# A four-layer graph network with an expert feed-forward part: the table's parts become the stationary operand, and the adjacency streams for four tiles at once

## The chip, the cores and the metric

One core of one Trainium2 chip. The metric is the device time of one execution in microseconds; the kernel before has a median of 3117.78 us over 3 runs (3117.64 to 3121.14). TensorE's matmuls are called PE here, its weight loads PEld, VectorE DVE, ScalarE ACT, GpSimd POOL and SyncE SP.

## The reference

6250 nodes with 256 features, 100000 edges (src, dst). Cut to what matters:

```python
deg = segment_sum(ones, rows) + 1.0;  dinv = rsqrt(deg)[:, None]
h = x @ W_in + b_in
for l in range(4):
    h_scaled = h * dinv
    msg = segment_sum(h_scaled[cols], rows) * dinv
    global_ctx = mean(h, axis=0) @ Wg[l] + bg[l]
    z = relu((h + msg) @ Wl[l] + bl[l] + global_ctx)
    h = (z - mu) * rsqrt(var + EPS) * gamma[l] + beta[l]
```

Behind it stands a feed-forward part: experts are chosen by a softmax of the mean row, two of eight are applied to every row (gelu between two products), then a layernorm. Both parts are added to x.

## The kernel before

**Tiles.** The nodes are T = 49 tiles of P = 128 rows. The gather and sum over edges is done as a product with a dense adjacency A, whose entries are small counts in fp8. A first stage (0 to 510 us) builds A from one-hot matmuls column by column of tiles, stages it in SBUF and writes it to DRAM (`write`, L539), counts degrees (`degrees`, L1491) and computes h = x @ W_in (`product`, L1529). Its last steps on PE are the degrees of column 48, the product and the mean row of tile 48; then DVE reads whether all counts fit (the flag), and the scales of the table follow.

**The table.** `tab` holds h times dinv in two f16 parts per tile, high (256 columns) and low (256 columns), for two layers in turn. ACT writes the high part (L1346 for the first layer, L1337 later), DVE the low part (L896) and raises `tab_ready`.

**The layers.** For each tile n of a layer, `aggregate` (L1628) on PE runs 49 matmuls, with a 128x128 fp8 block of A as the stationary operand (the weights) and 512 columns of `tab` (high and low) as the moving one, into one PSUM bank. The result has nodes on partitions. ACT copies its low half (L1367), DVE adds the halves, scales and adds the own term (h of the node itself) from the table (L982 to L988) into U. PE transposes U (`turn_u`, L1590), ACT and DVE split the transposed U in two f16 parts (L1369, L995), and PE multiplies by the layer's weights in six matmuls of 256 columns (`product_u`, L1598) into bank 4. In time, tile n's transposes stand at step 14 and its product at step 24 of the 49 steps of tile n+1. DVE then computes bias, relu and layernorm (L1004 to L1020), the sum of rows (L901) and the new table's low part (L896). In the last layer DVE writes h + x instead (L1029) and takes moments and a normalised row sum of the tile before (`moments`, `normal`, L948 and L958).

```python
for m in range(T):
    ...
    ins = mm(acc[a][:, :], A_s[:, a, m, :], tab[:, here + m, :], start=m == 0, stop=m == T - 1)
```

**What sets the order.** The order on each engine is written out by hand, with semaphores between engines. The first tile of a layer waits for the table; before its last step stands `mean` (L1608, four f32 matmuls), behind it `context` (L1620); in the first layer `mean` also waits for the bound of the layer weights (`wmax_set`). SP's queue first loads the layer weights (L551 to L554), then A's tiles, 784 KB each, into a ring of three buffers and one for the first tile (L563). Its requests are served in their order. Before the first product PE waits for `wx_ready`, which DVE raises when the layer weights are split in two f16 parts (L936 to L939). The routing behind the layers begins on PE at L1692 and L1695; L1695 waits for the last row sum of DVE.

Of the kernel before, what the change touches and what calls it, by code (L numbers as in the profile page):

```python
# [20 lines left out]
F16 = mybir.dt.float16  # L21
BF16 = mybir.dt.bfloat16
# [25 lines left out]
PK = 5  # L48
# [14 lines left out]
SEVEN = 7  # L63
assert T % SEVEN == 0
# [15 lines left out]
BEFORE_T, BEFORE_MM = 14, 24  # L80
# [28 lines left out]
def build(nc, x, src, dst, W_in, b_in, Wl, bl, Wg, bg, gamma, beta, Wr, br, W1, b1, W2, b2, fgamma, fbeta, out):  # L109
# [4 lines left out]
    AG = nc.dram_tensor("adjacency_general", [FIELDS * PK, PLANES, P, T, P], BF16).ap()  # L114
    ctx = ExitStack()
    with ctx:
# [53 lines left out]
        src_col = sb("src_col", [P, COLS])  # L170
        src_w = sb("src_w", [P, COLS])
# [5 lines left out]
        RW = 11136  # L177
# [32 lines left out]
        Abuf = work((RING + 1) * T * P // 4)  # L210
        A_s = Abuf.bitcast(F8).rearrange("p (a m s) -> p a m s", m=T, s=P)
        A32_s = Abuf.bitcast(I32).rearrange("p (a w) -> p a w", a=RING + 1)
        AG_s = Abuf.bitcast(BF16).rearrange("p (a m s) -> p a m s", m=T, s=P)
        U = work(RING * D).rearrange("p (a f) -> p a f", f=D)
        uT = work(D).bitcast(F16).rearrange("p (a k n) -> p a k n", k=KC, n=P)
        at[0] += (RING + 1) * D

        Wl_s = region[:, at[0]:at[0] + LAYERS * KC * D].rearrange("p (l k f) -> p l k f", l=LAYERS, k=KC)
        at[0] -= (RING + 1) * D
        gT = region[:, at[0]:at[0] + RING * SUPW].rearrange("p (b n) -> p b n", n=SUPW)  # L220
        gx = Abuf[:, 0:2 * TOP * FC * SUPW].bitcast(F16).rearrange("p (b a f n) -> p b a f n", b=2, a=2, n=SUPW)
        assert RING * SUPW <= (RING + 4) * D
        lo_f = work((RING + 1) * D).rearrange("p (a f) -> p a f", f=D)
        acc_s, hs, Q, Z, Zn, Zg, hf = (work(D) for _ in range(7))
        mean_s = work(D).rearrange("p (k n) -> p k n", k=KC)
        xb = work(RING * D).rearrange("p (a f) -> p a f", f=D)
        bg_s = region[:, (RING + 1) * T * P // 4:(RING + 1) * T * P // 4 + LAYERS * D].rearrange("p (l f) -> p l f", f=D)
        assert at[0] <= RW and LAYERS * D == (RING + 1) * D
        Wsq = U[:, 0:KC, :]

        xnb = sb("xnb", [P, D])
# [46 lines left out]
        c_read = sb("c_read", [P, T])  # L278
        c_own = sb("c_own", [P, T])
        c_back = sb("c_back", [P, LAYERS * T])  # L280
        node = sb("node", [P, T])
# [167 lines left out]
        block = ctx.enter_context(nc.Block())  # L449

        CX = 2
        CT = 9
        CE = 4
        CF = 8
        OUT_PER = [16 * (LOOP + 1), 16 * LOOP, 16 * LOOP]
# [1332 lines left out]
```

## Time and profile before

| | us |
|---|---|
| median of the runs | 3117.78 |
| the profiled execution, its own time | 3118.73 |
| its span, first to last instruction | 3117.1 |
| PE busy | 2988.8 |
| DVE busy | 1943.9 |
| ACT busy | 949.2 |
| mean granted clock of TensorE | 0.976 of full speed |

A PE matmul's duration (380 ns for 512 columns) is its latency; matmuls overlap, and the distance between starts is what a stream costs. A timeline row merges several instructions of a kind: its first number is the start, the second the length, xN the number of them, and in brackets stands the idle time before it with what ended it.

### The profile page before, as it was taken

How to read it: one execution, taken by the hardware profiler on the slowest of the kernel's cores; microseconds unless marked ns; L12 is line 12 of the kernel's file. 1: busy time of each engine (PE TensorE's matmuls, PEld its weight loads, DVE VectorE, ACT ScalarE, POOL GpSimd, SP SyncE). 2: the span in 40 equal slices, each digit the busy share in tenths (PEclk: the TensorE clock that was granted, in tenths of full speed). 3: DMA queues.
4: the chain of work that ended last, by engine and by line, in shares of the span. 5: the costliest groups of instructions: out<-in, count | busy, mean ns of one | idle time of the engine just before them, and what ended most of it. 6: DMA issues, size and time to landing. Idle time of an engine off the chain costs nothing.

```text
span 3117.1 us, 55195 instructions
## 1 busy us (share of the span) xinstructions
PE 2988.8 (96%) x18038; PEld 1702.5 (55%) x18038; DVE 1943.9 (62%) x5237; ACT 949.2 (30%) x2112; POOL 81.6 (3%) x169
## 2 busy tenths in 40 slices
PE   6999996999999999999999999999999999997998
PEld 5777774444444444444444444444444444445887
DVE  8999997555555555555554555545566666666776
ACT  5888897111111111111111111111111111116775
POOL 0000000000000000000000000000000000000111
PEclk9999997999999999999999999999999999998999
DMA  4333334222222221222212221222122222211000
GB/s 132 87 88 88 85 89 137 78 86 86 85 82 86 86 77 65 72 72 72 71 63 72 72 69 65 72 72 72 64 82 84 84 84 75 81 50 40 27 25 26
DMA packets 138138, 233.87 MB, mean 75 GB/s; under 512 B 13718, under 2 KB 105989, under 8 KB 138019
## 3 DMA queue, kind: packets, MB, share of 16 engines
q1 hardware_dynamic: 131058, 217.55, 21.5%
q10 hardware_dynamic: 4608, 8.39, 0.9%
q0 software_dynamic: 2352, 6.40, 0.7%
q8 instruction: 68, 1.11, 0.1%
q14 instruction: 52, 0.42, 0.0%
HBM read 186.58 MB, written 45.74 MB: 75 GB/s over the span
## 4 chain that ended last, share of the span: by engine, by line
PE 83%; ACT 10%; DVE 4%; issue 3%; DVEq 0%; ACTq 0%; DMA 0%; SPq 0%; POOL 0%; POOLq 0%
PE bank L1647 66%; ACT tab L1270 8%; PE bank L1605 4%; PE bank L1749 4%; PE bank L1732 4%; PE bank L1595 1%; PE bank L1495 1%; DVE later L812 1%; DVE region L779 1%; PE bank L1515 1%; PE bank L1541 1%; ACT later L1294 0%; ACT xnb L1288 0%; PE bank L1709 0%; PE bank L1526 0%
## 5 line engine op out<-in xcount | busy, mean ns | idle before, releaser
L1647 PE MATMUL bank<-tab,region 128*128 128x512 f16 x9604 | 2142.3, 380 | 15.8 <-DMA region<-adjacency 15.8
L1647 PEld LDWEIGHTS bank<-tab,region 128*128 128x128 fp8e4 x9604 | 940.6, 98 | 1066.2 <-DVE tab L896 18.0
L1270 ACT ACTIVATE tab<-later 128x539 fp8e4<-128x539 uint8 x588 | 336.2, 674 | 1.9 <-DVE later L812 1.9
L779 DVE TENSOR_SCALAR region<-iota_w,src_col,src_w 128x540 bf16<-128x540 int16 x858 | 310.5, 413 | 0.4 <-issue 0.2
L1373 ACT ACTIVATE sd<-mv,eps_c 128x1 f32<-128x1 f32 x196 | 57.7, 295 | 811.3 <-DVE mv L1011 811.3
L1004 DVE SCALAR_TENSOR_TENSOR region<-bank,c_back,later 128x256 f32<-128x256 f32 x196 | 94.8, 484 | 331.5 <-PE bank L1605 331.5
L995 DVE TENSOR_TENSOR region<-bank,region 128x256 f16<-128x256 f32 x196 | 83.2, 425 | 287.8 <-ACT region L1369 287.8
L1369 ACT ACTIVATE region<-bank 128x256 f16<-128x256 f32 x196 | 75.3, 384 | 568.1 <-PE bank L1595 568.1
L1367 ACT ACTIVATE region<-bank 128x256 f32<-128x256 f32 x196 | 75.3, 384 | 305.1 <-PE bank L1647 305.1
L1605 PE MATMUL bank<-later,region 128*128 128x256 f16 x1176 | 160.4, 273 | 0.9 <-DVE region L995 0.9
L1337 ACT ACTIVATE tab<-region,c_write 128x256 f32 (+1 forms) x147 | 74.6, 508 | 268.7 <-DVE region L1020 268.7
L1732 PE MATMUL bank<-tab 128*128 128x384 f16 (+1 forms) x816 | 139.0, 325 | 7.0 <-DVE tab L1126 4.6
L1605 PEld LDWEIGHTS bank<-later,region 128*128 128x128 f16 x1176 | 115.0, 98 | 56.0 <-DVE region L995 1.2
L1749 PE MATMUL bank<-tab,region 128*128 128x256 f16 (+1 forms) x1176 | 140.5, 277 | 0.0
L984 DVE TENSOR_TENSOR region<-bank,region 128x256 f32<-128x256 f32 x196 | 83.2, 425 | 86.9 <-ACT region L1367 86.9
L1515 PE MATMUL bank<-region 128*128 128x270 bf16 x900 | 132.8, 303 | 1.3 <-DVE region L763 0.8
L1515 PE MATMUL bank<-region,later 128*128 x864 | 125.8, 303 | 1.1 <-DVE region L779 1.1
L1749 PEld LDWEIGHTS bank<-tab,region 128*128 128x128 f16 (+1 forms) x1176 | 118.1, 101 | 15.1
L1515 PEld LDWEIGHTS bank<-region 128*128 128x128 f16 x900 | 109.9, 146 | 20.3 <-DVE region L779 1.6
L1515 PEld LDWEIGHTS bank<-region,later 128*128 128x128 f16 x864 | 111.4, 144 | 12.7 <-issue 1.6
L1137 DVE SCALAR_TENSOR_TENSOR region<-region,g_scale 128x384 f16<-128x384 f32 (+1 forms) x136 | 80.5, 594 | 54.4 <-ACT region L1440 54.2
L1732 PEld LDWEIGHTS bank<-tab 128*128 128x128 f16 x816 | 90.0, 114 | 43.8 <-issue 8.1
(235 smaller groups left out, 2425.1 us busy)
## 6 DMA issues: line engine op xcount, KB each, us to landing
region<-adjacency SPq DMA_DIRECT2D x196, 784.0 KB, 4.3
adjacency<-tab SPq DMA_DIRECT2D x12, 3136.0 KB, 13.7
region<-in_x POOLq DMA_DIRECT2D x48, 128.0 KB, 2.3
out<-region SPq DMA_DIRECT2D x48, 128.0 KB, 1.7
tab<-in_x SPq DMA_DIRECT2D x5, 1024.0 KB, 11.9
dstf<-in_L_ffn_W ACTq DMA_DIRECT2D x16, 256.0 KB, 2.6
srcf<-in_L_ffn_W ACTq DMA_DIRECT2D x16, 256.0 KB, 2.9
tab<-in_L_ffn_W SPq DMA_DIRECT2D x4, 512.0 KB, 4.8
```

Of the source, the lines that this page charges most:

```text
L779: v.tensor_scalar(hot_s[:, j, :], iota_w[:, 0:WP], src_col[:, ds(first_block[0] + j, 1)], src_w[:, ds(first_block[0] + j, 1)], ALU.is_equa ...
L984: tile_own.done(v.tensor_tensor(acc_s, acc[a][:, 0:D], lo_f[:, a, :], ALU.add))
L995: v.tensor_tensor(uT[:, 1, :, :], T3[3], uT[:, 0, :, :], ALU.subtract).then_inc(uT_split, 1)
L1004: tile_own.done(v.scalar_tensor_tensor(out=Z, in0=bank[4][:, 0:D], scalar=c_back[:, ds(n, 1)], in1=bias[:], op0=ALU.mult, op1=ALU.add))
L1137: v.scalar_tensor_tensor(out=gx[:, i % 2, 1, f, 0:w], in0=gT[:, q % RING, 0:w], scalar=g_scale[:, f // FC:f // FC + 1], in1=gx[:, i % 2, 0 ...
L1270: ins = a.activation(stage[h][:, :, slot, f * LANES:f * LANES + n], counts[:, :, 0:n], ACT.Copy, saturate=False)
L1367: a.activation(lo_f[:, s, :], acc[s][:, D:2 * D], ACT.Copy).then_inc(lo_ready, 1)
L1515: ins = mm(bank[k % 2 * 2 + half][:, 0:HALFP], hot_d[m % 2][:, :, j], hot_s[:, block + j, half * HALFP:(half + 1) * HALFP], start=j == 0, ...
L1605: ins = mm(bank[4][:, 0:D], uT[:, a, k, :], Wx[:, b, l, k, :], start=q == 0, stop=q == len(parts) - 1)
L1647: ins = mm(acc[a][:, :], A_s[:, a, m, :], tab[:, here + m, :], start=m == 0, stop=m == T - 1)
L1732: ins = mm(bank[q % RING][:, 0:w], W1x[:, b, f // FC * KC + k, f % FC:FF:FC], xfT[:, i % 2, c, k, 0:w], start=n == 0, stop=n == 3 * KC - 1)
L1749: ins = mm(bank[5 + u][0:r, 0:D], gx[:, i % 2, b, f, u * P:u * P + r], W2x[:, c, f // FC, f % FC, :], start=False, stop=n == 3 * TOP * FC - 1)
```

## The change

The numbers of a layer's 49 tiles are split in 14 groups: eleven of four tiles, one of three (44 to 46), and tiles 47 and 48 alone. For each group and each table tile m, PE now loads four 128x128 f16 blocks of `tab` (high and low part, two halves of the features) as weights and lets A move: for a group of four one instruction streams 4 x 128 columns of fp8, read as four pieces of 128 bytes at a distance of 896 bytes. The two feature halves collect in two banks, with features on partitions and nodes along the columns, so no transpose is needed before the product. Three pairs of banks are used in turn.

The own term goes into A's diagonal: DVE makes 49 blocks of A's diagonal block plus the degree plus one on the diagonal (`diagonal`), from a separate load of the 49 own blocks (`own_blocks`, pieces of 128 bytes), and the matmuls of a group's own tiles are cut around that block. ACT and DVE split a group's sums in two f16 parts, 512 columns at a time (`high_sums`, `split`), and the products of a group's tiles stand at fixed steps of the next group (`PRODUCTS_AT`). The products of the last five tiles, `mean` and `context` stand in the last groups and in the first group of the next layer.

A is loaded in seven chunks of seven column tiles for all tiles of a group, each as soon as its place is free (`a_used`); the chunks with a group's own tiles come last in that group (`chunk_order`). In the first group two chunks are requested ahead of the own blocks and the layer weights. At the end of the first stage the write of columns 44 to 47 is cut in two, the last product stands before the last degrees, and the first table tiles are made from tile 7 on, tiles 0 to 6 last. A few small DVE steps before the layers change (maxima by one reduction with absolute values, scales of the layers). The general path (for counts that don't fit) is changed in the same way and isn't run here.

The core of the diff:

```diff
+GROUP = 4
+STARTS = tuple(range(0, 48, GROUP)) + (47, 48)
+WIDTHS = (GROUP,) * 11 + (3, 1, 1)
+GROUPS = len(STARTS)
+PAIRED = (0, 1) * 6 + (2, 1)
+COLUMN = (0,) * 12 + (3, 0)
+LOOPED = 5
+PIECES = 32
+FULLEST = 2040.0
+BOUND_M, MEAN_M, CONTEXT_M = 30, 31, 36
+PRODUCTS_AT = {"first": {4: 48, 20: "mean", 24: "context"}, "four": {4: 0, 14: 1, 24: 2, 34: 3},
+               "three": {5: 0, 17: 1, 29: 2, 41: 3}, 12: {8: 44, 34: 45}, 13: {10: 46, 36: 47}}
...
+        sums = [[bank[0], bank[1]], [bank[2], bank[3]], [bank[6], bank[7]]]
+        def diag_of(t):
+            return diag_s[:, t, :] if t < T // 2 else diag_more[:, t - T // 2, :]
...
+        def chunk_order(g):
+            mine = sorted(set((STARTS[g] + d) // SEVEN for d in range(WIDTHS[g])))
+            return [c for c in range(T // SEVEN) if c not in mine] + mine
...
-            with sp.Fori(0, MLOOP) as i:
+                             stage32[h][:, :, slot:slot + width, :].rearrange("p t m s -> p t (m s)")).then_inc(a_written[h], 16)
+            with sp.Fori(0, MLOOP - 1) as i:
                 for h in range(2):
-                    write(h, i * (2 * MG) + h * MG, MG)
-            write(0, T - 1, 1)
+                    write(h, i * (2 * MG) + h * MG, 0, MG)
+            write(0, T - 1 - 2 * MG, 0, MG)
+            write(1, T - 1 - MG, 0, MG // 2)
+            write(1, T - 1 - MG // 2, MG // 2, MG // 2)
+            write(0, T - 1, 0, 1)
             sp.wait_ge(a_written[0], 16 * (MLOOP + 2))
-            sp.wait_ge(a_written[1], 16 * (MLOOP + 1))
+            sp.wait_ge(a_written[1], 16 * (MLOOP + 2))
...
+            def own_blocks():
+                blocks = bass.AP(tensor=A.tensor, offset=0, ap=[[T * P // 4, P], [(P * T + 1) * P // 4, T], [1, P // 4]])
+                sp.dma_start(own_a.bitcast(I32).rearrange("p (t w) -> p t w", w=P // 4), blocks).then_inc(own_in, 16)
             def fast():
-                layer_weights()
-                def one(l, n0, last):
-                    def load(n, t, i, a):
-                        sp.wait_ge(agg_done, n + 1)
-                        sp.dma_start(A32_s[:, a, :],
-                                     A[ds(t, 1), :, :, :].rearrange("o p m s -> (o p) (m s)")).then_inc(a_in[a], 16)
-                    tiles(sp, load, n0)
-                with sp.Fori(0, LAYERS) as l:
-                    one(l, l * T, False)
+                def load(gi, g, t0, w, c):
+                    sp.dma_start(A32_s[:, c, 0:w, :],
+                                 A[ds(t0, w), :, c * SEVEN:(c + 1) * SEVEN, :].rearrange("d p m s -> p d (m s)")
+                                 ).then_inc(a_in[c], 16)
+                def load_group(l, g):
+                    for c in chunk_order(g - 1 if g else GROUPS - 1):
+                        sp.wait_ge(a_used[c], l * GROUPS + g)
+                        load(l * GROUPS + g, g, STARTS[g], WIDTHS[g], c)
+                for c in chunk_order(0):
+                    load(0, 0, 0, GROUP, c)
+                    if c == chunk_order(0)[1]:
+                        own_blocks()
+                        layer_weights()
+                for g in range(1, GROUPS):
+                    load_group(0, g)
+                with sp.Fori(1, LAYERS) as l:
+                    for g in range(GROUPS):
+                        load_group(l, g)
...
+            for k in range(SEVEN):
+                first_low(k, T - SEVEN + k)
...
+            v.tensor_reduce(wbound[:, 0:LAYERS], Wl_s.rearrange("p l k f -> p l (k f)"), AX, ALU.max,
+                            apply_absolute_value=True).then_inc(wmax_set, 1)
+            def diagonal(t):
+                v.scalar_tensor_tensor(out=diag_of(t), in0=ident[:], scalar=degp[:, t:t + 1], in1=own_a8[:, t, :], op0=ALU.mult,
+                                       op1=ALU.add).then_inc(diag_ready, 1)
+            dve.wait_ge(own_in, 16)
+            for t in range(T // 2):
+                diagonal(t)
+            dve.wait_ge(s_rooted, 1)
...
+                def split(gi, pair, w, col):
+                    for k in range(KC):
+                        dve.wait_ge(s_high, gi * KC + (k + 1))
+                        v.scalar_tensor_tensor(out=sT[:, 1, k, col * P:(col + w) * P], in0=sums[pair][k][:, 0:w * P],
+                                               scalar=s_scale[:], in1=sT[:, 0, k, col * P:(col + w) * P], op0=ALU.mult,
+                                               op1=ALU.subtract).then_inc(s_low, 1)
...
-                    tile_own.done(v.tensor_tensor(hs, tab[:, here + t, 0:D], tab[:, here + t, D:2 * D], ALU.add))
-                    dve.wait_ge(lo_ready, n + 1)
-                    tile_own.done(v.tensor_tensor(acc_s, acc[a][:, 0:D], lo_f[:, a, :], ALU.add))
-                    tile_own.wait()
-                    tile_own.done(v.tensor_scalar(Q, acc_s, c_read[:, ds(t, 1)], None, ALU.mult))
-                    tile_own.wait()
-                    v.scalar_tensor_tensor(out=U[:, 0, :], in0=hs, scalar=c_own[:, ds(t, 1)], in1=Q, op0=ALU.mult,
-                                           op1=ALU.add).then_inc(u_ready, 1)
...
+                n0, t0 = l * T + STARTS[11], STARTS[11]
+                split(l * GROUPS + 11, PAIRED[11], WIDTHS[11], COLUMN[11])
+                norm(n0, t0, 11, 0)
+                norm(n0 + 1, t0 + 1, 11, 1)
+                split(l * GROUPS + 12, PAIRED[12], WIDTHS[12], COLUMN[12])
+                norm(n0 + 2, t0 + 2, 11, 2)
+                def last_split():
+                    split(l * GROUPS + 13, PAIRED[13], WIDTHS[13], COLUMN[13])
+                norm(n0 + 3, t0 + 3, 11, 3, last_split)
+                norm(n0 + 4, t0 + 4, 12, 0)
                 if last:
                     moments(T - 1)
...
+                def high_sums(gi, free, pair, w, col):
+                    act.wait_ge(agg_done, gi + 1)
+                    if not (isinstance(free, int) and free == 0):
+                        act.wait_ge(mm_done, free)
+                    for k in range(KC):
+                        a.activation(sT[:, 0, k, col * P:(col + w) * P], sums[pair][k][:, 0:w * P], ACT.Copy,
+                                     scale=s_scale[:]).then_inc(s_high, 1)
...
+            product(T - 1)
             degrees(T - 1, 2 * MG)
-            product(T - 1)
-            add_mean(T - 1, mean_last).then_inc(h0_summed, 1)
             clear(False).then_inc(deg_done, 1)
             pe.wait_ge(bad_set, 1)
             mm(bank[4][:, 0:1], ones[:], bad[:], start=True, stop=True).then_inc(bad_sum, 1)
+            add_mean(T - 1, mean_last).then_inc(h0_summed, 1)
...
-            def turn_u(n):
-                pe.wait_ge(u_ready, RING + n + 1)
-                pe.wait_ge(uT_split, n + 1)
-                for k in range(KC):
-                    ins = nc.tensor.transpose(T3[3][:, k, :], U[:, 0, k * P:(k + 1) * P], ident[:])
-                ins.then_inc(uT_done, 1)
...
+            def product_u(n, l, col):
+                if isinstance(n, int) and n == 0:
                     pe.wait_ge(wx_ready, 1)
-                pe.wait_ge(uT_split, n + 2)
+                pe.wait_ge(var_ready, n + 1)
                 parts = [(a, b, k) for a, b in ((0, 0), (0, 1), (1, 0)) for k in range(KC)]
                 for q, (a, b, k) in enumerate(parts):
-                    ins = mm(bank[4][:, 0:D], uT[:, a, k, :], Wx[:, b, l, k, :], start=q == 0, stop=q == len(parts) - 1)
+                    ins = mm(bank[4][:, 0:D], sT[:, a, k, col * P:(col + 1) * P], Wx[:, b, l, k, :], start=q == 0,
+                             stop=q == len(parts) - 1)
                 ins.then_inc(mm_done, 1)
...
+                def product_of(l, g, t):
+                    pe.wait_ge(s_low, 4 + (l * GROUPS + g + 1) * KC)
+                    product_u(l * T + t, l, COLUMN[g] + t - STARTS[g])
+                def between(l, g, q):
+                    if g == 0 and l == 0:
+                        if q == BOUND_M:
+                            weight_bound()
+                        elif q == MEAN_M:
+                            mean(0)
+                        elif q == CONTEXT_M:
+                            context(0)
+                    elif g == 0:
+                        what = PRODUCTS_AT["first"].get(q)
+                        if what == "mean":
                             mean(l)
-                        ins = mm(acc[a][:, :], A_s[:, a, m, :], tab[:, here + m, :], start=m == 0, stop=m == T - 1)
-                    ins.then_inc(agg_done, 1)
-                    if a == RING:
-                        context(l)
-                def rest(l):
-                    with pe.Fori(0, LOOP) as i:
-                        for a in range(RING):
-                            aggregate(l, l * T + i * RING + a + 1, a, i, l)
+                        elif what == "context":
+                            context(l)
+                        elif what is not None:
+                            product_of(l - 1, 13, what)
+                    elif g <= 11:
+                        what = PRODUCTS_AT["four" if g < 11 else "three"].get(q)
+                        if what is not None:
+                            product_of(l, g - 1, STARTS[g - 1] + what)
+                    else:
+                        what = PRODUCTS_AT[g].get(q)
+                        if what is not None:
+                            product_of(l, 11 if what < 47 else 12, what)
+                def done_after(order, q, c, w):
+                    rest = [m for m in order[q + 1:] if m // SEVEN == c]
+                    return not rest if w > 1 else rest == [order[-1]] or not rest and q < T - 1
+                def group(l, g):
+                    gi, t0, w, here = l * GROUPS + g, STARTS[g], WIDTHS[g], ((l + 1) & 1) * T
+                    to = sums[PAIRED[g]]
+                    if gi > 1:
+                        pe.wait_ge(s_low, 4 + (gi - 1) * KC)
+                    mine = range(t0, t0 + w)
+                    order = [m for c in chunk_order(g) for m in range(c * SEVEN, (c + 1) * SEVEN) if m not in mine] + list(mine)
+                    begun = set()
+                    for q, m in enumerate(order):
+                        between(l, g, q)
+                        c = m // SEVEN
+                        if c not in begun:
+                            begun.add(c)
+                            pe.wait_ge(a_in[c], (gi + 1) * 16)
+                        if gi == 0:
+                            pe.wait_ge(tab_ready, m - SEVEN + 1 if m >= SEVEN else T)
+                        elif g == 0 and (q == 0 or m >= STARTS[11]):
+                            pe.wait_ge(tab_ready, l * T + max(m + 1, STARTS[11]))
+                        own = m - t0 if t0 <= m < t0 + w else None
+                        if own is not None:
+                            pe.wait_ge(diag_ready, m + 1)
+                        for b in range(2):
+                            for k in range(KC):
+                                f = (b * KC + k) * P
+                                parts = [(A_s[:, c, 0:w, m % SEVEN, :], 0, w)]
+                                if own is not None:
+                                    parts = [(A_s[:, c, d0:d1, m % SEVEN, :], d0, d1)
+                                             for d0, d1 in ((0, own), (own + 1, w)) if d0 < d1]
+                                    parts.append((diag_of(m), own, own + 1))
+                                for moving, d0, d1 in parts:
+                                    ins = mm(to[k][:, d0 * P:d1 * P], tab[:, here + m, f:f + P], moving,
+                                             start=q == 0 and b == 0 and moving is parts[0][0],
+                                             stop=q == T - 1 and b == 1 and moving is parts[-1][0])
+                                    last = b == 1 and k == KC - 1
+                                    if last and q == T - 1 and d0 == own and d1 == own + 1 and moving is parts[-1][0]:
+                                        ins.then_inc(agg_done, 1)
+                                    elif last and done_after(order, q, c, w) and moving is (
+                                            parts[-1][0] if own is None else parts[-2][0]):
+                                        ins.then_inc(a_used[c], 1)
                 for l in range(LAYERS):
-                    aggregate(l, l * T, RING, 0, l - 1 if l else None)
-                    rest(l)
-                turn_u(LAYERS * T - 1)
-                product_u(LAYERS * T - 1, LAYERS - 1)
+                    for g in range(GROUPS):
+                        group(l, g)
+                product_of(LAYERS - 1, 13, T - 1)
```

## Rows read from the trace of the kernel before

**Rows 1.** Page: the chain's shares; costliest group: busy, mean ns, idle before.

```profile
PE 83%; ACT 10%; DVE 4%; issue 3%; DVEq 0%; ACTq 0%; DMA 0%; SPq 0%; POOL 0%; POOLq 0%
...
L1647 PE MATMUL bank<-tab,region 128*128 128x512 f16 x9604 | 2142.3, 380 | 15.8 <-DMA region<-adjacency 15.8
```

**Rows 2.** By stretch: busy us of each engine (instructions), clock, DMA share, GB/s.

```profile
510.00:560.00 50.00, 24.96 (x86) 11.90 (x86) 35.96 (x92) 23.59 (x58) 1.85 (x3) 0.65 0.52 148
...
600.00:1100.00 500.00, 500.00 (x2490) 245.81 (x2488) 272.01 (x683) 68.82 (x175) 0.00 (x0) 1.00 0.26 86
```

**Rows 3.** Timeline of PE, a steady tile: start, length, group.

```profile
562.69 8.58 PE L1647 MATMUL bank<-tab,region 128*128 128x512 f16 x39
571.10 0.38 PE L1595 MATMUL bank<-ident,region 128*128 128x128 f32 x2
571.32 2.32 PE L1647 MATMUL bank<-tab,region 128*128 128x512 f16 x10
573.48 0.82 PE L1605 MATMUL bank<-later,region 128*128 128x256 f16 x6
574.14 1.24 PE L1647 MATMUL bank<-tab,region 128*128 128x512 f16 x5
```

**Rows 4.** Timeline of PE, feed-forward part.

```profile
3062.73 2.78 PE L1749 MATMUL bank<-tab,region 128*128 128x256 f16 x24
3065.35 3.09 PE L1732 MATMUL bank<-tab 128*128 128x384 f16 x18
3068.27 0.60 PE L1709 MATMUL bank<-ident,layer_rows 128*128 128x128 f32 x4
...
3092.29 1.00 PE L1732 MATMUL bank<-tab 128*128 128x106 f16 x18
3093.13 0.27 PE L1745 MATMUL bank<-tab,ones_b 128*128 128x256 bf16 x1
```

**Rows 5.** Timeline of PE, from the last degrees to the first tiles.

```profile
507.64 1.45 PE L1495 MATMUL bank<-one_b,tab 128*128 128x1 bf16 x49 [3.26 <-ACT tab L1270]
...
530.73 12.53 PE L1647 MATMUL bank<-tab,region 128*128 128x512 f16 x48 [15.76 <-DMA region<-adjacency]
...
554.58 5.23 PE L1647 MATMUL bank<-tab,region 128*128 128x512 f16 x14
```

**Rows 6.** Timeline of PE, a layer's end.

```profile
1111.59 0.82 PE L1605 MATMUL bank<-later,region 128*128 128x256 f16 x6
...
1125.40 0.82 PE L1605 MATMUL bank<-later,region 128*128 128x256 f16 x6
```

**Rows 7.** Timeline of DVE: 512 columns, first and last step of a norm.

```profile
549.45 2.74 DVE L936 SCALAR_TENSOR_TENSOR later<-region,wscale,later 128x512 f16<-128x512 f32 x4
...
1009.49 0.48 DVE L1004 SCALAR_TENSOR_TENSOR region<-bank,c_back,later 128x256 f32<-128x256 f32 x1 [1.47 <-PE bank L1605]
...
1013.96 0.48 DVE L896 SCALAR_TENSOR_TENSOR tab<-region,c_write,tab 128x256 f32 x1 [0.34 <-ACT tab L1337]
```

**Rows 8.** Timeline of ACT and SP: first table, first loads of A.

```profile
518.38 19.65 ACT L1346 ACTIVATE tab<-tab,c_write  x49 [1.46 <-DVEq L882]
...
521.40 27.59 SPq L563 DMA_DIRECT2D region<-adjacency  x4
```

**Rows 9.** DMA packets from 511.5 to 516.2 us.

```profile
DMA packets 5420, 0.69 MB, mean 147 GB/s; under 512 B 5420, under 2 KB 5420, under 8 KB 5420
```

**Rows 10.** DMA packets from 518 to 527 us.

```profile
DMA packets 3205, 2.71 MB, mean 301 GB/s; under 512 B 1083, under 2 KB 3055, under 8 KB 3203
```

**Rows 11.** Page, DMA issues: queue, count, KB each, median us to landing.

```profile
region<-adjacency SPq DMA_DIRECT2D x196, 784.0 KB, 4.3
```

**Rows 12.** Timeline of PE and DVE, the end of layer 4.

```profile
2791.32 5.56 PE L1647 MATMUL bank<-tab,region 128*128 128x512 f16 x25
...
2805.80 0.43 DVE L952 BATCH_NORM_STATS2 st<-tab 128x6 f32<-128x256 f32 x1
...
2808.32 1.01 PE L1695 MATMUL bank<-mean_w,later 128*128 128x1 f32 x4 [4.09 <-DVEq L1046]
```

More of the change, by code:

```diff
@@ L938, in _ @@
             own.wait()
-            dve.sem_inc(wx_ready, 1)
             own.done(v.tensor_tensor(blg[:], blg[:], bg_s, ALU.add))
             own.wait()
+            for t in range(T // 2, T):
+                diagonal(t)
+            dve.wait_ge(diag_ready, T)
+            dve.sem_inc(wx_ready, 1)
             tile_own = Steps(dve, dve_tile)
@@ new lines, in split, with norm @@
+                def split(gi, pair, w, col):
[4 more added lines that the diff above has]
+                                               op1=ALU.subtract).then_inc(s_low, 1)
+                def norm(n, t, g, d, between=None):
+                    late = last and not (isinstance(t, int) and t == 0)
@@ L1271, in unpack @@
                                        saturate=False)
+                    if between and f == 4:
+                        between()
                 ins.then_inc(staged, 1)
@@ L1381, in one, with fetch, group @@
-                tiles(act, step, n0)
+                def fetch(q):
+                    act.wait_ge(scan_done, q * 2 + 2)
+                    for b, w in enumerate((W1, W2)):
+                        a.dma_start(scan_s[b], w.rearrange("e a b -> (e a b)").rearrange("(c p f) -> c p f", p=P, f=SCAN)[
+                            ds(q, 1), :, :].rearrange("o p f -> (o p) f")).then_inc(scan_in[b], 16)
+                def group(gi, n0, g, t0, pair, w, col, scan=False):
+                    if scan:
+                        fetch(2 * g)
+                    high_sums(gi, n0, pair, w, col)
+                    for d in range(w):
+                        norm(n0 + d, t0 + d)
+                        if scan and d == 1:
+                            fetch(2 * g + 1)
@@ new lines, in scanned @@
+                def scanned(*to):
+                    group(*to, scan=first)
+                one_group(scanned, l, 0)
+                one_group(scanned, l, 1)
+                looped_groups(act, scanned, l, 1, PIECES // (2 * GROUP))
+                for g in range(PIECES // GROUP, 2 * LOOPED + 1):
+                    one_group(group, l, g)
+                n0, t0 = l * T + STARTS[11], STARTS[11]
+                high_sums(l * GROUPS + 11, n0, PAIRED[11], WIDTHS[11], COLUMN[11])
+                norm(n0, t0)
@@ L1683, in general @@
+                    looped_groups(pe, group, l, 0, LOOPED)
+                    for g in range(2 * LOOPED, GROUPS):
+                        one_group(group, l, g)
                 for l in range(LAYERS):
```

366 lines of the change are left out of this document (206 added, 160 removed).

## The prediction

> **What bounds the kernel now.** I read the page first: PE is 83% of the chain that ended last, 66% of it in one line, the aggregation matmul L1647 [rows 1]. The table by stretch then splits the span. From 510 to 560 the building of A hands over to the layers with PE half idle; in the layers PE is busy 100%, all at a granted clock of 1.00, DVE 54%, ACT 14% [rows 2]. So there only PE time counts, whatever DVE and ACT do, as long as they don't get late.
>
> The timeline of PE in one steady tile gives the prices [rows 3]. 39 matmuls of 512 columns take 571.10 - 562.69 = 8.41 us, 216 ns each; two transposes of U 0.22 us (571.10 to 571.32); six product matmuls 0.66 us (573.48 to 574.14). 49 x 0.2157 + 0.22 + 0.66 = 11.45 us, the distance from tile to tile. In the feed-forward part 24 matmuls of 256 columns take 2.62 us (109 ns), 18 of 384 take 2.92 us (162 ns), 18 of 106 columns 0.84 us (46.7 ns) [rows 4]. All are columns at 2.4 GHz plus about 2.5 ns, the weights f16 or fp8: no weight load shows.
>
> Around the steady tiles: the first takes from 530.73 to 554.58, 23.85 us for 10.57 us of matmuls, with PE waiting for the table, the weights' bound and the context; behind it PE starts cold again, 14 matmuls in 5.23 us instead of 14 x 0.216 and a tail of 0.17, 3.2 [rows 3, 5]. At a layer's end the period is 1125.40 - 1111.59 = 13.81, 2.36 us over 11.45 [rows 6].
>
> **Part 1: table as weights, A moving.** The columns stay: before 49 x 49 matmuls of 512 per layer; after, per table tile, four weight blocks (two halves of the features, high and low) times 128 columns for each tile of a group, 49 x 49 x 4 x 128 again. Their number changes. A group of four: 45 x 4 of 512 columns (180 x 0.2157 = 38.8), and for its own four tiles, where the diagonal block is cut out, per weight block 384+128, 128+256+128 twice, 384+128 columns; at 56 (46.7 ns plus 22 columns), 109 and 162 ns that is 0.88 us, times four 3.5. Sum 42.3 us. The group of three: 184 x 0.162 + 2.0 = 31.8. Each single tile: 196 x 0.056 = 10.95. A layer: 11 x 42.3 + 31.8 + 21.9 = 519.2 us against 49 x 10.57 = 517.9: **+5.2 us** over four.
>
> Two things in this no row shows. First, 196 matmuls of 128 columns in a row: there are 18 in a row at the full rate, and 49 of one column in 1.45 us, 30 ns each, right behind a wait [rows 4, 5]. I take 56 ns, next to the 46.7; the upper bound is the 109 ns of 256 columns. The Trainium skill, "TensorE: Matmul & The Clock Gate", section "Back-to-back issue gap", speaks against this: a stream of pairs of weight load and matmul is said to take about 81 ns each at N=128. By it 1568 matmuls in single groups would cost 25 ns more each, 40 us, and the sum be 3102. The same passage gives 131 ns for N=512, where this trace has 216.
>
> Second, a moving operand in fp8, read as four pieces of 128 bytes that lie 896 bytes apart. Bounds: nothing (a column is a column), or every joint costs what a new matmul costs, 3 x 2.5 ns. I take nothing, the value of every kind of operand in rows 3 and 4.
>
> **Part 2: the sums come out transposed.** The two transposes go: 195 x 0.22 = **-42.9 us**. The product's six matmuls stay (195 x 0.66 = 128.7 on both sides). On DVE five steps a tile (L982 to L995) go, and two splits of a group's 512 columns come, 0.69 us each by the 512-column form (2.74 us for four) [rows 7]. A tile's norm takes 4.95 us (L1004 at 1009.49 to L896's end) and has 10 x 0.864 + 0.66 = 9.3: hidden, also in the last layer with 2.5 us on top [rows 12]. A group's first product waits for its splits: two steps of ACT, taken as long as DVE's, and DVE's second behind them, 3 x 0.69 + 0.3 of hand-overs = 2.4 us, and stands at 4 x 0.864 = 3.5 us: hidden. Behind group 11 it stands only 8 x 0.225 = 1.8 us in, and two splits of 384 columns take about 2.1: 0.3 us, **+1.2** over four layers.
>
> **Part 3: the start.** Before, product and mean row stand behind the last degrees (507.64), then flag, root and scales follow, ACT writes the first table tile at 518.38; A's first block is requested at 521.40, behind 2.5 MB of weights, and PE starts at 530.73 [rows 5, 8, 10]. After, the product precedes the degrees, some 4 us less: scales near 514.3. What is late next is the write of A. The last one, 6272 pieces of 128 bytes, starts only when the 512-byte one ahead of it has drained; its own packets take 4.7 us or a little more (5420 of them are seen in 511.5 to 516.2) [rows 9]. With the one ahead cut in two and half of it gone earlier, it starts 1.1 us after its issue: landed at about 515.1. SP requests chunk 1 of A at 516.0, 1.3 us to the first packet, 0.46 MB at 301 GB/s [rows 10]: 518.8, and PE starts at **519.2 instead of 530.7, -11.5 us**. The table is written at 0.40 us a tile by ACT (19.65 for 49 [rows 8]), PE takes one per 0.864: no wait. In the first group 2.1 us of cold clock and bound, mean and context (0.25 + 0.55 + 0.97 = 1.8) remain; 13.3 us (23.85 - 10.57) and the second cold start (2.2) go.
>
> Behind chunks 1 and 2 come the own blocks, 6272 pieces of 128 bytes, then the weights. By rows 9 and 10 they take 4.7 us (that was a write; a read may take more) and 2.56 MB at 301 GB/s, 8.5 us, so chunk 3 lands near 536, and PE wants it at 519.2 + 2.1 + 14 x 0.864 = 533.4: **+3 us**; bounds 0, and 10 if the pieces take twice as long. The DVE chain to wx_ready (table to 539, reduction 2.7, 24 diagonals, roots, splits, 25 diagonals, each about 0.28, half a 256-column step) ends near 567, before group 1 wants it at 572. Hidden; 5 us late would cost nothing.
>
> **Part 4: layer ends.** Mean and context stand at steps 20 and 24 of the next group, the late tiles' rows are wanted at step 37 only: 1.5 us instead of 2.36 with its idle. Three times: 7.1 before, 4.6 after, with the first group's 1.8 that is 6.4. A's pieces: a group of four loads 3.2 MB in 42 us, as now 0.8 MB in 11.45, which lands in 4.3 us [rows 11]. The tight place is the first group of a layer, whose chunks a single tile frees within 11 us; chunk 1 is free 3.1 us into it, needs under 6 us behind chunk 0, and is wanted at 11. Hidden; SP has nothing else queued there.
>
> **Part 5: the end of layer 4.** DVE needs per tile the norm without its last hand-over to ACT and L896, 4.1 us, and 2.4 of moments and normal (2805.80 to PE's release at 2808.32) [rows 7, 12]; tiles 44 to 48 come within the 25 us of two single groups. From the start of group 12: 1.9 (split) + 2.4 (moments of 43) + 5 x 6.5 + 1.6 (two splits) + 0.9 (hand-overs) = 39.3, where PE is done at 24.8: 14.5 us from the last matmul to L1695, against 2808.32 - 2796.88 = 11.4 now. **+3.0 us**. What follows is unchanged.
>
> **Sum.** Before, 530.73 to 2796.88: 2071.7 (196 x 10.57) + 13.3 + 2.2 + 128.7 + 42.9 + 7.1 = 2265.9 (2266.2 in the trace). After: 2071.7 + 5.2 + 128.7 + 6.4 + 2.1 + 1.2 + 3 = 2218.3. So -47.6 - 11.5 + 3.0 = -56.1. The profiled execution took 3118.7: 3062.6; the median of the runs shown lies 1 us below it: **3062 us**.
>
> **Rivals.** (a) *Short matmuls are not paced by their columns*, but by issue or weight load. For it: no run of more than 18 is shown; against it those 18, and the 49 at 30 ns. Halfway between 56 and 109 ns the single groups lose 1568 x 27 ns = 42 us: 3104; at 109 ns 83 us, slower than before. Chance 0.11.
> (b) *The moving read in four pieces is slower.* One place, each of 2164 wide matmuls a layer, 8656 in all: from 56 / 8656 = 6.5 ns each it eats the gain; with 2.5 ns at each of three joints it is 7.5 ns, 65 us: 3127, slower. For it: no row shows such a read. Against: no operand shown costs anything. The Trainium skill, same page, section "Weight-path perf modes", has fp8 at bf16 speed; no run here shows it for a moving operand. Chance 0.09.
> (c) *The edges don't shrink*: own blocks and weights hold chunk 3 until 545, and at each layer's end the norms of tiles 44 to 48 or a late chunk hold PE for 4 us: 10 + 16 = 26 us less gain, 3088. For it: the order in which SP issues; against: the rates of rows 9 to 11. Chance 0.11.
> (d) *It doesn't do what it says*: the start and first tile stay as they are, 24.8 us of gain missing, 3087. For it: the table is still built by the same steps; against: loads no longer stand behind the weights. Chance 0.03.
> Forecast: 0.66, itself 3052 to 3075.
>
> The range 3050 to 3105 holds the forecast and most of (a), (c), (d). What a measurement can tell from no change is 0.2%, 6 us: faster 0.87, same 0.03, slower 0.10 ((b) and the top of (a)).
>
> **What would show it.** 216 ns per 512 columns and 56 per 128, so single groups of 11 us; 42.3 us plus four products from group to group; PE's start near 519, a gap of 0 to 10 us at chunk 3; L1695's counterpart 14 us behind the last matmul. Wrong if wide matmuls come every 223 ns or more, single groups take 16 us, or PE idles at layer ends.

## The result and the profile after

The changed kernel takes 3074.83 us (median, 3073.42 to 3075.79, 4 runs) against 3118.82 for the kernel before on the same chip: ratio 0.9858, 95% interval 0.9841 to 0.9875, 44 us faster. The forecast was 3062 us, 56 us faster: right in sign and inside its range, 12 us short of the gain that was forecast.

The page of the profiled execution (3074.75 us, against 3118.73 before), its first line, the chain and the costliest group, answers to [rows 1]:

```profile
span 3073.1 us, 54692 instructions
...
PE 82%; ACT 9%; DVE 4%; issue 2%; DMA 1%; SPq 1%; DVEq 1%; POOL 0%; ACTq 0%; POOLq 0%
...
L1850 PE MATMUL bank<-region,tab 128*128 128x512 fp8e4 (+4 forms) x11712 | 2118.1, 339 | 21.5 <-DMA region<-adjacency 21.5
```

PE is still the chain. New is the end of the last line: 21.5 us of idle that a DMA of A ended, where [rows 1] had 15.8, all of it at the start. The table by stretch (busy us of each engine, granted clock, DMA share, GB/s) shows the same against [rows 2]: the hand-over is fuller, 39.3 instead of 25.0 us of PE in 510 to 560, and the layers, 100% busy before, now have a hole.

```profile
510.00:560.00 50.00, 39.31 (x168) 17.58 (x168) 41.39 (x113) 23.10 (x57) 0.00 (x0) 0.85 0.72 188
600.00:1100.00 500.00, 497.27 (x3024) 268.84 (x3023) 206.73 (x517) 51.79 (x118) 0.00 (x0) 1.00 0.31 86
```

The timeline of PE, two stretches: a product and forty wide matmuls up to the next product, and the same in a single group with 104 short ones (start, length, group).

```profile
572.16 0.82 PE L1760 MATMUL bank<-later,region 128*128 128x256 f16 x6
572.82 8.80 PE L1850 MATMUL bank<-region,tab 128*128 128x512 fp8e4 x40
581.45 0.82 PE L1760 MATMUL bank<-later,region 128*128 128x256 f16 x6
```

```profile
1072.94 5.97 PE L1850 MATMUL bank<-region,tab 128*128 128x128 fp8e4 x104
1078.75 0.82 PE L1760 MATMUL bank<-later,region 128*128 128x256 f16 x6
```

(581.45 - 572.82) / 40 = 215.8 ns for 512 columns of fp8 in four pieces, the 215.7 of [rows 3] with an f16 operand in one piece. (1078.75 - 1072.94) / 104 = 55.9 ns for 128 columns, 104 in a row.

The same timeline at the start of the first group and at the start of group 2 in the first layer; the last row is SP's, of the same stretch (the request of A's chunks in group 2's order).

```profile
518.05 13.97 PE L1850 MATMUL bank<-region,tab 128*128 128x512 fp8e4 x56 [7.30 <-DMA region<-adjacency]
535.41 15.55 PE L1850 MATMUL bank<-region,tab 128*128 128x512 fp8e4 x64 [3.39 <-DMA region<-adjacency]
...
616.51 5.30 PE L1850 MATMUL bank<-region,tab 128*128 128x512 fp8e4 x16 [2.66 <-DMA region<-adjacency]
621.65 0.82 PE L1760 MATMUL bank<-later,region 128*128 128x256 f16 x6
```

```profile
612.96 1.24 SPq L600 DMA_DIRECT2D region<-adjacency  x2
```

Read them so: PE starts at 518.05 (530.73 in [rows 5]), stands 3.4 us in front of chunk 3, and again 2.7 us at 613.8, the end of group 1. The chunk that it waits for was requested at 612.96, 0.7 us before PE wanted it, and such a load takes 3.4 us:

```profile
region<-adjacency SPq DMA_DIRECT2D x308, 448.0 KB, 3.4
```

The same wait ends at 1174.4, 1730.8 and 2287.1 in the later layers, once a layer. Behind the first one the clock was at half speed (1.2 GHz) for a while, as it was not behind the second: mean granted clock of 5.5 us from the restart.

```profile
616.50:622.00 5.50, 5.49 (x20) 2.32 (x21) 0.00 (x0) 0.00 (x0) 0.00 (x0) 0.69 0.13 44
1174.40:1179.90 5.50, 5.46 (x29) 2.82 (x30) 0.90 (x3) 0.00 (x0) 0.00 (x0) 1.00 0.11 37
```

And the end of layer 4, which answers to [rows 12]:

```profile
2748.26 3.07 PE L1850 MATMUL bank<-region,tab 128*128 128x128 fp8e4 x52
2753.07 0.83 PE L1760 MATMUL bank<-later,region 128*128 128x256 f16 x6 [1.74 <-DVE region L1069]
...
2763.94 1.01 PE L1908 MATMUL bank<-mean_w,later 128*128 128x1 f32 x4 [6.80 <-DVEq L1156]
```

From the end of the last aggregation matmul (2751.33) to the first matmul of the mean row (2763.94) pass 12.6 us, before 11.4.

**The budget.** Start -12.7 us (518.05 against 530.73); first to last aggregation matmul 2233.3 against 2266.2, -32.9; end +1.2; the rest of the span +0.4. The sum is -44.0, by which the two profiled executions differ. The start is less certain than it looks. Five more runs below have the same code ahead of it, and PE's first aggregation matmul lies between 517.99 and 521.20 in them, as the first stage ends sooner or later; by these the start is worth 9.5 to 13 us.

### The profile page after: what moved, and what is told of

Same layout as the page of the kernel before. It is cut to its first block, busy times and chain, and to the rows that moved or that the text cites. A ratio compares the mean times of both kernels' runs of the same rounds, so it can differ in the third digit from the quotient of the medians.

```text
span 3073.1 us, 54692 instructions
## 1 busy us (share of the span) xinstructions
PE 2948.7 (96%) x20138; PEld 1781.4 (58%) x20138; DVE 1630.1 (53%) x4410; ACT 868.9 (28%) x1834; POOL 81.5 (3%) x169
## 4 chain that ended last, share of the span: by engine, by line
PE 82%; ACT 9%; DVE 4%; issue 2%; DMA 1%; SPq 1%; DVEq 1%; POOL 0%; ACTq 0%; POOLq 0%
PE bank L1850 66%; ACT tab L1380 8%; PE bank L1760 4%; PE bank L1962 4%; PE bank L1945 4%; DVE region L839 1%; PE bank L1658 1%; PE bank L1678 1%; DVE later L872 1%; DMA region<-adjacency 1%; PE bank L1704 1%; ACT later L1406 0%; PE bank L1922 0%; PE bank L1689 0%; DVEq L814 0%
## 5 line engine op out<-in xcount | busy, mean ns | idle before, releaser
L1850 PE MATMUL bank<-region,tab 128*128 128x512 fp8e4 (+4 forms) x11712 | 2118.1, 339 | 21.5 <-DMA region<-adjacency 21.5
L1850 PEld LDWEIGHTS bank<-region,tab 128*128 128x128 f16 x11712 | 1050.0, 98 | 994.5 <-DMA region<-adjacency 11.9
L1069 DVE SCALAR_TENSOR_TENSOR region<-bank,s_scale,region 128x512 f16<-128x512 f32 (+2 forms) x112 | 71.4, 680 | 479.3 <-ACT region L1498 479.3
L839 DVE TENSOR_SCALAR region<-iota_w,src_at 128x540 bf16<-128x540 int16 x858 | 310.9, 415 | 0.5 <-PE bank L1678 0.2
L1498 ACT ACTIVATE region<-bank,s_scale 128x512 f16<-128x512 f32 (+2 forms) x112 | 64.9, 630 | 470.2 <-PE bank L1850 470.0
L1598 ACT ACTIVATE region<-bank,b_s,e_sel 128x384 f32<-128x384 f32 (+1 forms) x136 | 88.0, 647 | 67.2 <-PE bank L1945 66.5
L971 DVE SCALAR_TENSOR_TENSOR later<-region,valid,later 128x256 f32<-128x256 f32 x196 | 95.0, 484 | 17.0 <-DVE region L1098 5.7
```

The lines of the kernel that those rows point to most:

```text
L839: v.tensor_scalar(hot_s[:, j, :], iota_w[:, 0:WP], src_col[:, ds(first_block[0] + j, 1)], src_w[:, ds(first_block[0] + j, 1)], ALU.is_equa ...
L971: return v.scalar_tensor_tensor(out=hsum[:], in0=h, scalar=valid[:, ds(t, 1)], in1=hsum[:], op0=ALU.mult, op1=ALU.add)
L1598: a.activation(gT[:, q % RING, 0:w], bank[q % RING][:, 0:w], ACT.Gelu, bias=b1_s[:, e, f % FC:f % FC + 1], scale=e_sel[:, e, 2:3]).then_in ...
L1850: ins = mm(to[k][:, d0 * P:d1 * P], tab[:, here + m, f:f + P], moving, start=q == 0 and b == 0 and moving is parts[0][0], stop=q == T - 1 ...
```

## The experiments

Each ran beside the kernel before on one chip, and a ratio is to that kernel there; its median lay between 3118.24 and 3118.82 us each time, so medians are compared across experiments too.

**1. Another order of the chunks in group 2.** Group 1's own tiles, 4 to 7, lie in chunks 0 and 1. Own tiles come last, so chunk 0 is held to the end of group 1, and group 2 asks for it first.

```diff
             mine = sorted(set((STARTS[g] + d) // SEVEN for d in range(WIDTHS[g])))
+            if g == 2:
+                return [2, 0, 3, 4, 5, 6, 1]
```

Expected:

> The changed kernel with one group's chunks in another order: group 2 (tiles 8 to 11) takes them as 2, 0, 3, 4, 5, 6, 1 instead of 0, 2, 3, 4, 5, 6, 1; the loads follow by their own rule. Theory (release order): group 1's own tiles lie in chunks 0 and 1, so both are freed last, and chunk 0 is what group 2 asks for first; its load of 448 KB (3.4 us) starts too late. The four waits of 2.7 us at the start of group 2 go, and the cold clock behind the first of them (1.7 us): 12.5 us less than the changed kernel, 3062 us. Rival (rate): chunks in pieces of 896 bytes land too slowly whenever a group of four follows; then the wait only moves to another chunk of groups 2 or 3, and the time is 3072 to 3075.

Measured: 3060.32 us (3059.59 to 3066.1), ratio 0.9823, interval 0.9809 to 0.9836; 14.5 us under the changed kernel. The list of waits for A's DMA (total, times, longest) of the changed kernel and of this one:

```profile
PE bank L1850 <- DMA region<-adjacency: 21.5, 6, 7.3
```

```profile
PE bank L1852 <- DMA region<-adjacency: 9.4, 2, 7.2
```

Six waits became two, those of the start. Bytes, pieces and their number are as they were. The release order was the cause, and the rate of loads was not. Some 2 us of the 14.5 are the start's, where the edit changes nothing: in this profile PE's first 120 matmuls and the wait for chunk 3 between them take 30.9 us instead of 32.8, because that wait is 2.1 us instead of 3.4 and PE comes out of it at full clock (ahead of it PE has 1.0 us more of half clock). Behind that stretch the layers are 13.1 us shorter, near the 12.5 expected.

**2. Three chunks ahead of own blocks and weights, on top of 1.**

```diff
-                    if c == chunk_order(0)[1]:
+                    if c == chunk_order(0)[2]:
                         own_blocks()
                         layer_weights()
```

Expected:

> As the run with the other order in group 2, and in the first group three chunks instead of two are requested ahead of the own blocks and the layer weights. Theory: the 3.4 us wait for chunk 3 and the second cold start behind it (1.6 us) go, 5 us less again: 3057 us, with chunk 4 wanted at 538 and landed near 534. Rival: own blocks and weights fill the queue as before and the wait moves to chunk 4, or weights that land 1.5 us later hold the chain to wx_ready: 3061 to 3063.

Measured: 3055.58 us (3053.69 to 3058.78), ratio 0.9806, interval 0.9793 to 0.982. This is the fastest version, 1.9% under the kernel before and 19 us under the changed one. Its timeline of PE has the first group in one piece:

```profile
517.99 27.70 PE L1852 MATMUL bank<-region,tab 128*128 128x512 fp8e4 x120 [6.85 <-DMA region<-adjacency]
545.53 0.28 PE L1776 MATMUL bank<-wbound,ones 128*128 128x5 f32 x2
```

No wait moved to chunk 4 or to the product of tile 0. The step over experiment 1, 4.7 us, is near the 5 expected; the two intervals overlap, the vanished row is what shows it. From PE's first to its last aggregation matmul the two profiles differ by 3.4 us (2218.3 and 2214.9); another 1.35 us lie ahead of PE's start (519.34 and 517.99), which the edit doesn't touch.

**3. The two transposes put back.** Two f32 transposes of 128 columns stand ahead of every product; they write into a part of the bank that nobody reads.

```diff
                 pe.wait_ge(var_ready, n + 1)
+                for k in range(KC):
+                    nc.tensor.transpose(bank[4][:, D + k * P:D + (k + 1) * P], ident[:], ident[:])
                 parts = [(a, b, k) ...
```

Expected:

> The changed kernel with two f32 transposes of 128 columns added ahead of every product (their result is not used), as many as the change took away. Theory: in the layers only PE's own time counts, so 196 x 0.22 = 43 us come back: 3118 us. Rival: PE has slack behind the waits for A and the splits, and part of the gain is theirs: under 35 us more, below 3110.

Measured: 3118.99 us (3115.35 to 3122.59), ratio 1.0003, interval 0.9994 to 1.0012: the 44 us are gone. In its timeline they take their 0.22 us, in front of the product:

```profile
1010.85 0.38 PE L1759 MATMUL bank<-ident 128*128 128x128 f32 x2
1011.07 0.82 PE L1762 MATMUL bank<-later,region 128*128 128x256 f16 x6
```

From PE's first to its last aggregation matmul this profile has 2277.3 us, the changed kernel's 2233.3: 44.0 more. So 43 us of transposes are worth 43 to 44 us, and everything else in the change came to about nothing as it stood. By the rows the start with its first tile and the layer ends gave some 22 us; the waits at group 2 (13 us), the larger number of matmuls (5, as forecast) and the end (1) took most of it.

**4. The kernel before with A's first load ahead of the layer weights.**

```diff
-                layer_weights()
...
+                        load(n0, 0, 0, RING)
+                        layer_weights()
```

Expected:

> The kernel before, with the load of A's first tile ahead of the layer weights, nothing else. Theory (a group of four covers the table): with one tile as the first piece of work, its end hangs on the table (542) and the chain of DVE and ACT to the context (552.7), not on A's arrival: PE starts some 9 us earlier and the second tile at the same time; 3117 to 3119 us, no gain. Rival (the start counts by itself): 8 to 9 us less, 3110.

Measured: 3116.74 us (3114.79 to 3121.76), ratio 0.9999, interval 0.999 to 1.0008: no difference. Its timeline of PE:

```profile
521.41 5.38 PE L1653 MATMUL bank<-tab,region 128*128 128x512 f16 x14 [6.73 <-DMA region<-adjacency]
527.09 2.76 PE L1653 MATMUL bank<-tab,region 128*128 128x512 f16 x7 [0.29 <-DVE tab L902]
...
542.54 0.68 PE L1618 MATMUL bank<-ident,later 128*128 128x128 f32 x4 [0.52 <-DVEq L921]
547.57 0.59 PE L1624 MATMUL bank<-wbound,ones 128*128 128x4 f32 x2 [4.35 <-DVE wbound L930]
...
552.63 2.08 PE L1630 MATMUL bank<-later,region 128*128 128x256 f32 x4 [4.02 <-ACT region L1369]
554.50 4.24 PE L1653 MATMUL bank<-tab,region 128*128 128x512 f16 x14
```

PE starts 9.3 us earlier and then goes at the table's pace; the second tile starts at 554.50, before at 554.58 [rows 5]. So the early start alone gives nothing here: one tile has 10.6 us of work, and the table takes 22. A group of four has 42 us of work for the same time. That it is the group that lets the early start count is an argument from these rows; no run has the changed kernel with a late start.

**5. The kernel before with the new end of the first stage.**

```diff
+            product(T - 1)
             degrees(T - 1, 2 * MG)
-            product(T - 1)
-            add_mean(T - 1, mean_last).then_inc(h0_summed, 1)
...
+            add_mean(T - 1, mean_last).then_inc(h0_summed, 1)
...
-            with sp.Fori(0, MLOOP) as i:
+            with sp.Fori(0, MLOOP - 1) as i:
...
-            write(0, T - 1, 1)
+            write(0, T - 1 - 2 * MG, 0, MG)
+            write(1, T - 1 - MG, 0, MG // 2)
+            write(1, T - 1 - MG // 2, MG // 2, MG // 2)
+            write(0, T - 1, 0, 1)
```

Expected:

> The kernel before with the end of its first stage as in the changed kernel: last product ahead of the last degrees, the write of columns 44 to 47 cut in two. Theory: flag, scales and table start about 4.6 us earlier (513.7 against 518.4 in the traces), the chain to the first tile's end is made of the table and the steps behind it, so all of it comes through: 3114 us. Rival: A's arrival behind the weights (530.7) holds the start and the first tile's end takes it back: 3117 to 3119.

Measured: 3114.69 us (3111.11 to 3120.59), ratio 0.9989, interval 0.998 to 0.9998: some 3.5 us, the number expected, though the interval nearly touches no change. The theory behind the number is borne out only in part. The table starts 1.6 us earlier (516.75, before 518.38) and not 4.7, because in this kernel its start waits for the write of A (ACT's row, the table's first steps; then PE's of the second tile):

```profile
516.75 13.67 ACT L1352 ACTIVATE tab<-tab,c_write  x34 [1.47 <-DMA adjacency<-tab]
```

```profile
552.93 3.83 PE L1653 MATMUL bank<-tab,region 128*128 128x512 f16 x14
```

The second tile starts 1.65 us earlier (554.58 in [rows 5]), so what the table gained comes through. The other 1.4 us that this profile shows are the clock behind that restart: 14 matmuls in 3.83 us, before in 5.23. Nothing in the edit explains that, so it may be chance.

**6. Every wide matmul of A in pieces of 128 columns, on top of 2.**

```diff
-                                parts = [(A_s[:, c, 0:w, m % SEVEN, :], 0, w)]
+                                parts = [(A_s[:, c, d:d + 1, m % SEVEN, :], d, d + 1) for d in range(w)]
```

Expected:

> The kernel with group 2's new order and three chunks first, with every wide matmul of A (four tiles, 512 columns, or three, 384) cut in matmuls of 128 columns with their own weight load: 25232 matmuls more, the same columns. Theory (columns plus some 2.5 ns each): 66 us more than that kernel's 3055.6, 3121 us. Rival (a stream of short pairs costs 81 ns each, paced by issue, weight load or instruction supply): over 800 us more, near 3900. In between if only the supply of instructions falls behind: over 3150.

Measured: 3120.95 us (3117.7 to 3125.16), ratio 1.0011, interval 1.0001 to 1.002: 65.4 us over experiment 2, 2.6 ns for each of 25232 more matmuls. Its PE lines by form, and 160 such matmuls in a row up to the next product:

```profile
L1852 PE MATMUL bank<-region,tab 128*128 128x128 fp8e4 x35808 | 2102.6, 219 | 6.8 <-DMA region<-adjacency 6.8
```

```profile
579.46 9.10 PE L1852 MATMUL bank<-region,tab 128*128 128x128 fp8e4 x160
588.39 0.82 PE L1762 MATMUL bank<-later,region 128*128 128x256 f16 x6
```

(588.39 - 579.46) / 160 = 55.8 ns, each with a weight load of its own, and there are 35808 of them, 2 ms in all. Rival (a) is out. For the price of the short groups the choice between 56 ns and the Trainium skill's 81 ns ("TensorE: Matmul & The Clock Gate", section "Back-to-back issue gap") is settled by this run.

**7. Loads asked for in the order 0 to 6, on top of 2.** It undoes the rule that loads are asked for in the order in which their places come free; the groups of four stay.

```diff
-                    for c in chunk_order(g - 1 if g else GROUPS - 1):
+                    for c in range(T // SEVEN):
```

Expected:

> The kernel with group 2's new order and three chunks first, but the loads of A are asked for in the order 0 to 6 instead of the order in which their places come free. Theory: SP's queue stands at the first chunk that is not free. In group 0 that is chunk 0, free only at its end, so all loads of group 1 start then and its first chunk (2) lands third: 5.9 us of wait and 1.7 of cold clock; in group 1 chunk 1 blocks and chunk 2 lands second behind it: 4.6 and 1.7. Other groups' late chunks are wanted 12 us into the next group or later. Four layers: 42 us without the cold clock, 56 with it, so 3098 to 3111 us. Rival: the loads are fast enough in any order: 3056 to 3060.

Measured: 3131.05 us (3126.69 to 3132.14), ratio 1.0037, interval 1.0024 to 1.0051: 75 us over experiment 2, and slower than the kernel before. The mechanism is right, the size was 20 to 33 us too small. The waits, and the restart behind one of them with SP's requests ahead of it (1140.80 is the last matmul of group 0 in the second layer):

```profile
PE bank L1852 <- DMA region<-adjacency: 62.3, 9, 8.6
```

```profile
1140.80 0.22 PE L1852 MATMUL bank<-src_at,tab 128*128 128x128 f16 x1
1147.18 5.10 PE L1852 MATMUL bank<-region,tab 128*128 128x512 fp8e4 x16 [6.16 <-DMA region<-adjacency]
```

```profile
1140.99 5.04 SPq L602 DMA_DIRECT2D region<-adjacency  x7
```

Without the one at the start there are eight waits of 55 us in all, behind groups 0 and 1 of each layer, 6.9 each where 5.25 was expected: seven requests take SP 5.04 us to issue, and PE, which wants the third chunk first, restarts 6.2 us behind the first request. Some 17 us more are the clock. The 16 matmuls behind each of the eight restarts take 5.10 to 6.24 us, where at full clock they take 3.62; that is 1.5 to 2.6 us each, 17.0 in all, against 14 expected. Waits and clock together are the 74 us by which this profile is longer than experiment 2's between PE's first and last aggregation matmul (2289.3 against 2214.9). The stretch from the restart shown, 1147.1 to 1152.6, has a mean granted clock of 0.72:

```profile
1147.10:1152.60 5.50, 5.42 (x21) 2.38 (x22) 0.00 (x0) 0.00 (x0) 0.00 (x0) 0.72 0.84 290
```

## Why the prediction was right in sign and 12 us short

**Part 1, columns** held. 215.8 ns for the moving fp8 in four pieces (forecast 215.7), 55.9 ns for 128 columns (forecast 56). Group 1 with its four products takes 45.0 us (568.71 to 613.70), as summed: 42.3 and four times 0.66. Rivals (a) and (b) are refuted by these rows, (a) also by experiment 6. The Trainium skill's sentence that fp8 runs at bf16 speed without the mode that it calls DoubleRow ("TensorE: Matmul & The Clock Gate", section "Weight-path perf modes") now has a trace for a moving operand that agrees: 215.8 ns here, 215.7 for f16 in [rows 3].

**Part 2, transposes** held: -42.9 forecast, 44 us when put back (experiment 3). The splits never held PE back behind the groups of four. Behind group 11 the product starts 0.29 us after the matmul ahead of it (2728.15 to 2728.44) and not 0.06: 0.23 us in each of the four layers, where 0.3 was priced.

**Part 3, start** held: 518.05 for 519.2, and the wait for chunk 3 was 3.4 us for 3. That it fits to the microsecond is partly luck, as the same start lies between 517.99 and 521.20 in the other runs. What it missed is that PE restarts cold behind that wait, some 1.6 us. Experiment 4 shows that the order of the loads alone doesn't give this gain.

**Part 4 failed, in one sentence:** "The tight place is the first group of a layer". I looked where the chunks are freed fastest. The tight place is where a chunk is freed last and wanted first. A group of four in chunks of seven lies in one chunk or in two; with two, both are held nearly to its end. In group 1 these are 0 and 1, and group 2 begins with 0. Each wait costs 2.8 us beyond the normal distance of starts (2.88, 2.89, 3.02 and 2.90 less 0.056), 11.5 in all, and 1.7 of cold clock behind the first (16 matmuls in 5.30 us instead of 3.62): 13.2 us. Behind the first group, and behind the other groups that hold two chunks (3, 5, 8 and 10), the next group begins with a chunk that has long been free. Experiment 1 changed the order alone and got 14.5 back, 13.1 of them in the layers behind the start. The rule for it stood in `chunk_order` and could have been written down for 14 groups in a table: position of release, position of use.

**Part 5, the end,** was mis-sized: +3.0 forecast, +1.2 measured. From the start of group 12 the chain of DVE takes 37.3 us where 39.3 were summed: 6.4 us a tile for 6.5, two one-tile splits of 0.6 for 0.8, and less for hand-overs.

In sum, -56.1 forecast; +13.2 for group 2, +1.6 cold start at chunk 3, -1.2 from the earlier start, -1.8 from the end, and small terms: -44.0. No term of the sum and no rival had the wait at group 2; that the time stayed inside the range is owed to the room left there for rivals. Rival (c), the edges don't shrink, had the right kind (a late chunk that holds PE once a layer) at the wrong edge and with 26 us.

## What to carry to other kernels

When a buffer is freed piece by piece and refilled by an in-order queue, write the order of release of one round against the order of use of the next for every round, not for the typical one: one piece that is last in the first list and first in the second costs most of its load each time (2.8 of 3.4 us here). Swapping which operand stays in TensorE costs nothing per column here (215.8 against 215.7 ns for 512), so the choice can be made by which layout the next step wants; that saved the two transposes of every tile. An earlier start of the bottleneck engine gave nothing where its first piece of work was shorter than the chain beside it (experiment 4), so compare the two before moving the start.

## What the runs showed of the hardware

- The clock's answer to a short wait is not the same each time: behind waits of 2.7 us the granted clock stayed at 1.00 in three layers and fell in one, and in experiment 3, with the same four waits, it fell behind two (16 matmuls in 5.06 and 5.30 us, twice in 3.61). Behind the eight waits of 6.2 to 8.6 us in experiment 7 it fell every time and cost 17 us, as much as a third of the waits again.
- Behind the request of 6272 pieces of 128 bytes (L595, the own blocks) SP's next one (L588) stands 7.18 us (column two), and 7.2 to 7.5 in the five other runs with the same sequence; in the kernel before, where nothing like it stands ahead, the same request takes 0.36. How much of that is due to the two or three chunks ahead of it isn't separated. Requests that a bottleneck waits for should not stand behind such a one.

```profile
515.04 0.51 SPq L595 DMA_DIRECT2D region<-adjacency  x1
515.59 7.18 SPq L588 DMA_DIRECT2D region<-in_L_gnn_bg  x1
522.81 0.44 SPq L589 DMA_DIRECT2D region<-in_L_gnn_Wl  x1
```

- Reading such pieces from DRAM took 217 GB/s (518.6 to 522, nearly all of the packets 128 bytes) against 147 for the write [rows 9].

```profile
DMA packets 5533, 0.74 MB, mean 217 GB/s; under 512 B 5503, under 2 KB 5532, under 8 KB 5532
```
